# Folding Wv and Wo of each head into one matrix, once a layer, in a stack of local-attention layers

## The reference

```python
def attn_layer(x, Wqkv, qs, ksc, Wo):
    q, k, v = jnp.split(x @ Wqkv, 3, -1)          # each 16 heads of 64
    q = l2norm(q) * qs; k = l2norm(k) * ksc       # then rotary tables on both
    out = local_attention(q, k, v)                # softmax(q k^T * 8, masked) @ v, per window
    out = out.transpose(0, 2, 1, 3).reshape(b, n, INNER)
    return out @ Wo                               # 1024 -> 128
def ffn_layer(x, g, bln, W1, b1, W2, b2): ...     # layernorm, x @ W1, a * gelu(gate) @ W2
```

## Time and profile before

| | |
|---|---|
| median of three runs | 4001.08 us (3993.65 to 4002.0) |
| profiled execution | 4002.27 us, span 4000.5 us |
| PE busy | 3733.8 us (93%) |
| DVE busy | 3151.4 us (79%) |
| ACT busy | 2570.7 us (64%) |
| POOL busy | 2781.7 us (70%) |
| PE busy from 2000 to 3000 us | 971.03 of 1000 us, granted clock 1.00 |

### The profile page before, as it was taken

How to read it: one execution, slowest core, us unless ns; L and a number is a source line. 1 busy time by engine, 2 the same in 40 slices (tenths; PEclk the granted TensorE clock), 3 DMA queues, 4 the chain that set the end, 5 groups by cost and what they waited for, 6 DMA issues and landing times. The chain is left out here.

```text
span 4000.5 us, 109740 instructions
## 1 busy us (share of the span) xinstructions
PE 3733.8 (93%) x42284; PEld 2927.6 (73%) x42284; DVE 3151.4 (79%) x4328; ACT 2570.7 (64%) x3589; POOL 2781.7 (70%) x2249
## 2 busy tenths in 40 slices
PE   6998897799999999999999999999999999999996
PEld 4766675677777777777777777777777777777774
DVE  4666664888888888888888888888888888888884
ACT  3555554566666666666666666666666767676763
POOL 2554552777777777777777777777777777777772
PEclk9999998999999999999999999999999999999998
DMA  1122110322223222232222232222322223222222
GB/s 42 59 74 73 66 68 13 100 66 60 62 63 100 66 58 64 55 103 63 68 53 66 82 79 64 61 61 62 102 66 62 60 60 99 62 70 54 68 54 62
DMA packets 157178, 267.01 MB, mean 67 GB/s; under 512 B 32062, under 2 KB 51644, under 8 KB 152380
## 3 DMA queue, kind: packets, MB, share of 16 engines
q1 hardware_dynamic: 157116, 266.19, 24.7%
HBM read 44.81 MB, written 26.21 MB: 18 GB/s over the span
## 5 line engine op out<-in xcount | busy, mean ns | idle before, releaser
L826 POOL TENSOR_TENSOR st_qk_rot<-st_qk_rot,st_qk_sq 128x1024 f32<-128x1024 f32 x384 | 920.5, 2402 | 692.7 <-DVE st_qk_sq L728 692.7
L455 PE MATMUL st_ps<-st_wqkv,st_xs 128*128 128x512 f32 x3456 | 949.6, 410 | 25.8 <-issue 18.3
L455 PEld LDWEIGHTS st_ps<-st_wqkv,st_xs 128*128 128x128 f32 x3456 | 608.2, 189 | 194.6 <-issue 75.2
L846 POOL TENSOR_TENSOR st_qk_rot<-st_qk_rot,st_rn 128x1024 f32<-128x1024 f32 x384 | 723.1, 1904 | 15.0
L710 DVE TENSOR_REDUCE st_nt<-st_qk_sq 128x16 f32<-128x1024 f32 x384 | 466.2, 1214 | 234.6 <-ACT st_qk_sq L573 233.2
L728 DVE TENSOR_TENSOR st_qk_sq<-st_ps,st_rot 128x512 f32<-128x512 f32 x768 | 490.1, 678 | 0.0
L714 DVE TENSOR_TENSOR st_qk_rot<-st_ps,st_rot 128x1024 f32<-128x1024 f32 x384 | 466.1, 1214 | 9.8 <-PE st_ps L472 9.8
L472 PE MATMUL st_ps<-consts_sb,st_qk_rot 128*128 128x128 f32 x3072 | 402.2, 274 | 27.9 <-DVE st_hid L802 14.9
L571 ACT ACTIVATE st_qk_sq<-st_ps 128x512 f32<-128x512 f32 x192 | 115.0, 599 | 486.3 <-PE st_ps L455 485.8
L472 PEld LDWEIGHTS st_ps<-consts_sb,st_qk_rot 128*128 128x128 f32 x3072 | 355.8, 141 | 94.1 <-DVE st_hid L802 34.7
L465 PEld LDWEIGHTS st_ps<-st_oT,st_wo 128*128 128x128 f32 x3072 | 368.8, 192 | 69.5 <-issue 67.7
(11 more groups left out here) (144 smaller groups left out, 6944.8 us busy)
## 6 DMA issues: line engine op xcount, KB each, us to landing
st_v_bd<-st_v_tok SPq DMA_DIRECT2D x1152, 128.0 KB, 2.4
st_v_bd<-st_v_tok SPq DMA_DIRECT2D x672, 64.0 KB, 2.1
wqkv_parts<-at_w_parts SPq DMA_DIRECT2D x18, 1024.0 KB, 4.6
st_wqkv<-wqkv_parts SPq DMA_DIRECT2D x18, 1024.0 KB, 7.0
at_w_raw<-in_wqkv SPq DMA_DIRECT2D x18, 512.0 KB, 5.1
rotary_tables<-at_rot SPq DMA_DIRECT2D x6, 512.0 KB, 3.4
st_rot<-rotary_tables SPq DMA_DIRECT2D x24, 128.0 KB, 2.4
st_wo<-in_wo SPq DMA_DIRECT2D x6, 512.0 KB, 4.4
```

Of the source, the lines that this page charges most:

```text
L455: last = pe.matmul(out[:, c * 512:(c + 1) * 512], xs[:, x_part, t * P:(t + 1) * P], rhs, start=(n == 0), stop=(n == len(PASSES) - 1))
L826: pool.tensor_tensor(qk_rot[:, cols], qk_rot[:, cols], qk_sq[:, cols], ALU.add).then_inc(rot_done[a], 1)
L846: pool.tensor_tensor(view, view, rn[:, par, heads_of(a)].unsqueeze(2).to_broadcast([P, HEADS, DH]), ALU.mult).then_inc(normed[a], 1)
```

## The change

In the first attention, once a layer: v's piece of `Wqkv` is no longer split by POOL but transposed by TensorE (`vt`, two jobs), copied by ACT, multiplied per head with that head's rows of `Wo` (`fold`, four jobs of four products with 64 rows), and split by ACT (high part) and DVE (remainder). The result for each head is 128 x 128, so v becomes 16 x 128 = 2048 columns wide, `v0` (first head of each pair) and `v1` (second head).

In the stack: two value projections instead of one; `spread_v` moves twice the bytes in the same number of DMAs; the softmax weights are multiplied with their reciprocal sums in SBUF by DVE (new L727) before they are transposed; `z` is now weights times the folded values, summed over the eight pairs of heads in PSUM (32 products of 128 columns, as `o` had); it is copied by ACT (128 x 128) and transposed in one instruction (`zt`). The jobs `o`, `ot` and the old `z` are gone, and with them L792 and the copy of oT. The output side of a tile comes three tiles back, and the order and banks of the jobs are new.

```diff
-            feed = {3: [(("m1", -1, 0), (1,))], 0: [(("m2", -2, 0), (1,))], 1: [], 2: [(("y", -2, 0), (1,))]}[t]
+            feed = {3: [(("m1", -1, 0), (5,))], 0: [(("m2", -2, 0), (5,))], 1: [], 2: [(("y", -2, 0), (5,))]}[t]
-            return [tile("q", 0, 0, 1), tile("tq", 1, 2, 3), tile("k", 0, 4, 5), tile("tk", 1, 6, 7),
-                    tile("v", 0, 2, 3), tile("ot", 3, 0, 1), tile("sim", 1, 6, 7), tile("pt", 2, 2, 3), *feed,
-                    tile("z", 3, 0), tile("o", 2, 4, 5), *hidden]
+            return [tile("q", 0, 0, 1), tile("pt", 3, 2, 3), tile("k", 0, 4, 5), tile("z", 3, 6), tile("tq", 1, 2, 3),
+                    tile("tk", 1, 6, 7), tile("v0", 0, 2, 3), tile("v1", 0, 0, 1), tile("sim", 1, 6, 7), *feed,
+                    tile("zt", 3, 4), *hidden]
...
-                            elif kind == "z":
-                                pe.wait_ge(taken["ot"], tiles_done(u, d, index))
-                                for c in range(IC):
-                                    last = pe.matmul(out[:, 0:P], wo[:, c, :], oT[:, c * P:(c + 1) * P], ...)
+                            elif kind == "zt":
+                                pe.wait_ge(taken["z"], tiles_done(u, d, index))
+                                last = pe.transpose(out[:, 0:P], z_tok[:, :], ident)
...
-                            elif kind == "o":
+                            elif kind == "z":
                                 pe.wait_ge(taken["pt"], tiles_done(u, d, index))
-                                            out[g * WIN:(g + 1) * WIN, c * P:(c + 1) * P],
+                                            out[g * WIN:(g + 1) * WIN, 0:P],
                                             probT[:, c * P + g * WIN:c * P + (g + 1) * WIN],
-                                            v_bd[:, par, g, :, c * DH:(c + 1) * DH], start=True, stop=True)
+                                            v_win[:, par, g, c * P:(c + 1) * P], start=(c == 0), stop=(c == IC - 1))
...
 # ACT, behind the copies of qT and k_bd; the exponential, probT and z_tok now stand before them
                         if alive(u, 0):
+                            copy_v(0)
+                            reciprocal_norm()
+                            copy_v(1)
                         if t == 2 and alive(u, 1):
                             round_half(u, 1, 0)
...
 # DVE, behind the rotations and the remainder
+                        if alive(u, d2):
+                            weights = s[:, t2 % 2, :].rearrange("p (h k) -> p h k", h=HEADS)
+                            dve.tensor_reduce(den[:, t2 % 2, 0, :], weights, AX.X, ALU.add).then_inc(den_ready, 1)
+                            dve.reciprocal(den[:, t2 % 2, 1, :], den[:, t2 % 2, 0, :]).then_inc(den_ready, 1)
+                            dve.tensor_tensor(weights, weights, den[:, t2 % 2, 1, :].unsqueeze(2).to_broadcast([P, HEADS, 2 * WIN]),
+                                              ALU.mult).then_inc(scaled, 1)
...
-                            dve.wait_ge(ready["z"], n - 3)
+                            dve.wait_ge(ready["zt"], n - 3)
-                            dve.tensor_tensor(
-                                o[:, :].rearrange("p (h d) -> p h d", h=HEADS), slot_of("o", d2, t2)...,
-                                den[:, t2 % 2, 1, :].unsqueeze(2).to_broadcast([P, HEADS, DH]), ALU.mult).then_inc(taken["o"], 1)
...
 # the first attention, TensorE
+                    elif kind == "fold":
+                        rows, half = slice(g // 2 * DH, (g // 2 + 1) * DH), g % 2
+                        for i in range(TILES):
+                            c = TILES * half + i
+                            last = pe.matmul(out[:, i * P:(i + 1) * P], wvT[rows, c, :], wo_l[rows, c, :], start=True, stop=True)
```

More of the change, by code:

```diff
@@ L393, in unit @@
                             load_w12(layer)
-                        if what == "wqkv" and t == TILES - 1:
-                            for kind in "qkv":
-                                sp.wait_ge(ready[kind], tiles_done(u, 0, t))
+                        if what == "wqkv" and t >= TILES - 2:
+                            for kind in (("q", "k"), ("v0", "v1"))[t - (TILES - 2)]:
+                                sp.wait_ge(ready[kind], tiles_done(u, 0, TILES - 1))
                                 load_wqkv(layer + 1, kind)
@@ L406, in layer_loads @@
                     u0 = layer * BATCH
-                    unit(u0, layer, None if first else "wo")
+                    unit(u0, layer)
                     unit(u0 + 1, layer, None if first else "w12")
@@ L411, in layer_loads @@
                     unit(u0 + (BATCH - 1), layer, None if last else "wqkv")
-                for kind in "qkv":
+                for kind in PROJ:
                     load_wqkv(0, kind)
@@ L547, in round_half @@
                     if alive(u, d - 1):
-                        act.wait_ge(ready["v"], tiles_done(u, d - 1, 2 * half + 1))
+                        act.wait_ge(ready["v1"], tiles_done(u, d - 1, 2 * half + 1))
                     cols = slice(half * 2 * P, (half + 1) * 2 * P)
@@ L809, in _ @@
             def _(pool):
-                pool.memset(v_bd[:, :, :, :, :], 0.0).then_inc(v_zeroed, 1)
-                pool.wait_ge(v_zeroed, 1)
-                pool.sem_inc(ready["o"], 2)
+                for a in range(2):
+                    pool.memset(v_win[a * 2 * WIN:a * 2 * WIN + WIN, 0, 0, :], 0.0).then_inc(v_zeroed, 1)
+                pool.wait_ge(v_zeroed, 2)
+                pool.sem_inc(ready["z"], 2)
                 pool.wait_ge(small_in, 64)
@@ L1074, in _ @@
             def _(pe):
+                for kind in ("vt", "fold"):
+                    pe.sem_inc(ready[kind], PER[kind])
+                    pe.sem_inc(taken[kind], PER[kind])
+                pe.sem_inc(fold_high, PER["fold"])
                 pe.wait_ge(w_in, 80)
@@ L1179, in m_product @@
                             last = pe.matmul(out[:, :], wo[:, r, :], aT[:, r, :], start=(r == 0), stop=(r == GROUPS - 1))
+                    elif kind == "vt":
+                        pe.wait_ge(raw_in, (b - 1) * 48 + 16)
+                        for i in range(TILES):
+                            at = (TILES * g + i) * P
+                            last = pe.transpose(out[:, i * P:(i + 1) * P], w_raw[:, at:at + P], ident)
+                    elif kind == "fold":
+                        rows, half = slice(g // 2 * DH, (g // 2 + 1) * DH), g % 2
+                        pe.wait_ge(taken["vt"], count(b, 0, 2, half))
+                        pe.wait_ge(fold_in, (b - 1) * 16 + 16)
+                        for i in range(TILES):
+                            c = TILES * half + i
+                            last = pe.matmul(out[:, i * P:(i + 1) * P], wvT[rows, c, :], wo_l[rows, c, :],
+                                             start=True, stop=True)
                     elif kind == "x":
@@ L1199, in m_products @@
                     for job in jobs_at(s, part):
-                        if alive(b, job[1]):
+                        if job_alive(b, job[0], job[1]):
                             m_product(b, job)
```

229 lines of the change are left out of this document (116 added, 113 removed), and 4 rows, old and new, of the table M_JOBS.

## The result

Four runs of the changed kernel took 5059.73 to 5077.93 us, median 5073.16 us; the kernel before took 4000.73 us beside them. The ratio is 1.268, interval [1.265, 1.271]: 27% slower. The forecast was 4900 us with a range to 5090. The profiled execution took 5059.73 us, span 5057.9 us.

The account below looks back on a forecast made before the run. TensorE set the pace before; after, a closed loop of DVE and TensorE would. 4002 + 780 (loop and waits for POOL) + 86 (clock) + 30 (first attention) = 4898, rounded 4900 us; range 4430 to 5090, own 4810 to 5010.

Parts of the forecast that it names:

- The closed loop: In the stack, TensorE's k waits for DVE's addition to x, DVE's cosine product (T0) for tq; tile 3 +1.6 us.
- The wait for POOL: DVE's new product stands until POOL's running instruction ends, then takes 1.1 us; with the loop, 780 us for 48 units.
- ACT's late rounding: In tiles 0 and 2 ACT rounds later, delaying DVE's remainder; 1.0 us each without the waits for POOL.
- Rival 2: The loop closes, but DVE's products do not wait for POOL and the clock holds: 4454 us, chance 0.2.
- TensorE's clock: Idle gaps in tiles 0 and 2 lower TensorE's clock: one fall a unit at 1.8 us, 86 us, bounds 0 to 259.
- Rival 3: The clock falls in three loops of every unit of the stack: 5071 us, chance 0.14.
- Two of my signs: In the profile after, TensorE's busy share in the stack near 70%, and DVE idle 2 to 3 us before T0.
- The rest: First attention's added instructions on TensorE, +30 us; spreads and weight loads at layer changes taken at nothing.
- rival 1: TensorE stays the bound in the stack and the loop does not close: 3825 us, faster, chance 0.05.

## Why the prediction was right, and where it was off

The direction and the mechanism held; one term was mis-sized.

- **The closed loop** held: T0 is released by tq in all four tiles, and k waits for the addition in tiles 0, 2 and 3. Tile 1 goes by the h products, as forecast. DVE's legs, T0 to the addition's end, are 13.14 us in tile 3 (predicted 13.14), 15.89 in tile 0 (16.15) and 17.65 in tile 2 (18.1); tile 1's loop is 21.79 (22.5), as POOL was not late there: the mask was through 10.8 us after T0, not 11.4. That the loop is a cause and not only a picture is shown by the orders that open it: tq second takes 364 us off, and with the early rounding and tk ahead of z on top 550.
- **The wait for POOL** held: mean 2.36 us instead of 1.2, ends 1.1 after POOL's, and ACT's late rounding cost what was worked out (0.86 idle, remainder 1.88). The replacement by a reduction took 311 us off, the early rounding 320. These overlap and are not to be added. Rival 2 is out.
- **TensorE's clock** was the step that was off. I counted one fall a unit, at 1.8 us, 86 us. The three legs of TensorE sum to 20.3 us a unit against 3 x 4.5, 6.8 more, 325 us in 48 units; with the gaps filled at least 214 us of that went. A fall also costs more than the 1.8 us that I had: 3.0, 1.75 and 2.0 us in tiles 0, 2 and 3. Rival 3 had the count of falls right: its three loops with a fall are the ones measured. That its total of 5071 us lies 2 us from the median is luck: its falls were too cheap by 66 us, and its DVE legs and tile 1 too long by 67. I had no reason for one fall in place of three: the gaps that I worked out myself were there (before pt in tile 0 4.2 us, measured 4.32; before k in tile 3 2.8, measured 2.58). Only the one before k in tile 0, over 2 us in my sum, was 0.86, because the clock was down already and pt took 1.94 us instead of 1.06. Two of my signs were off by the same cause: TensorE is busy for 78% and not near 70%, since slower passes count as busy, and DVE idles 2.8 to 6.3 us before T0, not 2 to 3.
- **The rest**: the stack starts 32 us later where I had 30, and with the drain and the ends of the stack 22 us lie outside the loops. The spreads cost nothing, as taken, although their landing time doubled.

By terms: 4898 from the forecast, plus 325 - 86 for the clock, less 1.4 us a unit (67 us) for DVE's legs and tile 1, less 8 for the rest, gives 5062; the profiled execution took 5059.73.

By the count of its passes TensorE has less to do, as rival 1 had it; no run shows what that alone is worth. It did not count here, because TensorE stopped being the bound.

## What to carry to other kernels

Before counting what a busy engine saves, follow the banks and single buffers once around: if an engine's job waits for another engine's last step and that one's first step waits for the job, the loop costs the sum of both legs, whatever either is busy. A gap that such a loop opens on TensorE can be paid twice, the second time in the clock of what follows, as in three of four tiles here, and filling one of two gaps gave nothing back. And move one edge at a time with the next edge named: most reorderings here opened one wait and met the next, and two gains of over 300 us each made 317 together.
